# Decays of a gated delta-rule layer by a running product on VectorE, and VectorE's dependent steps in another order

## The reference

```python
q = silu(conv4(x @ Wq.T)); k, v = silu(conv4(x @ Wk.T)), silu(conv4(x @ Wv.T))   # k, v: two per token
beta = 2 * sigmoid(x @ Wb.T)
g = -exp(A_log) * softplus(x @ Wa.T + dt_bias)      # one per token and head, on the first of its two keys
q, k = l2norm(q) / sqrt(128), l2norm(k)
def step(state, inp):                                # 128 steps
    state = state * exp(g_t)
    v_new = (v_t - k_t @ state) * b_t
    state = state + outer(k_t, v_new)
    return state, q_t @ state                        # kept for the second key of a token
o = rms_norm(o) * o_norm_w * silu(x @ Wg.T)
return o.reshape(B, L, KEY_DIM) @ Wo.T
```

## Time and profile before

| | us |
|---|---|
| three runs, median | 1167.6 |
| lowest, highest | 1165.88, 1169.84 |
| profiled execution: its span | 1164.1 |

### The profile page before, as it was taken

The page is one execution under the profiler, slowest core; times in us unless marked ns, Lnnn a source line. Parts: engine busy times, 40 slices in busy tenths (PEclk is TensorE's granted clock), DMA queues, the critical chain, the costliest instruction groups (busy, mean ns, idle before and its releaser), DMA issues.

```text
span 1164.1 us, 28733 instructions
## 1 busy us (share of the span) xinstructions
PE 1114.7 (96%) x11460; PEld 768.8 (66%) x11460; DVE 821.3 (71%) x1452; ACT 703.5 (60%) x1215; POOL 501.4 (43%) x709
## 2 busy tenths in 40 slices
PE   8989799999999999999997899889999999999998
PEld 3444455555555555565554556679999899989987
DVE  5989668868868778778767665676566666565562
ACT  5767477667677676776775866645444444444443
POOL 1659475685684783883975812212000000011000
PEclk9999799999999999999999999999999999999999
DMA  4222234545545555565555642252222221111100
GB/s 124 61 54 69 69 55 78 98 98 73 117 80 75 109 82 94 103 121 123 120 84 145 190 133 75 44 175 49 52 51 52 69 52 47 47 46 48 30 20 10
DMA packets 147284, 93.74 MB, mean 81 GB/s; under 512 B 80688, under 2 KB 130736, under 8 KB 146256
## 3 DMA queue, kind: packets, MB, share of 16 engines
q1 hardware_dynamic: 146000, 91.71, 35.8%
q10 hardware_dynamic: 1152, 0.21, 0.1%
HBM read 54.77 MB, written 14.55 MB: 60 GB/s over the span
## 4 chain that ended last, share of the span: by engine, by line
PE 76%; DVE 10%; POOL 5%; ACT 4%; issue 3%; SPq 1%; DMA 1%; ACTq 0%; DVEq 0%; POOLq 0%
PE proj L535 21%; PE out L1673 5%; PE gram L550 5%; PE turned_v_chain L1673 5%; PE proj L1735 4%; PE turned_v_chain L1747 4%; DVE conv L1143 4%; PE proj L1612 4%; PE gram L1647 2%; PE turned_v_chain L541 2%; PE out L559 2%; POOL inverse L1378 2%; PE decays L566 2%; POOL rank_one L1375 2%; PE turned_v_chain L684 2%
## 5 line engine op out<-in xcount | busy, mean ns | idle before, releaser
L1143 DVE SCALAR_TENSOR_TENSOR conv<-proj,kq_weights,conv 128x504 f32<-128x504 f32 (+2 forms) x261 | 189.8, 732 | 25.8 <-ACT conv L865 19.3
L535 PE MATMUL proj<-xT,vg_weights 128*128 128x512 f32 x384 | 189.8, 618 | 4.8 <-DVE conv L1143 2.0
L1990 POOL TENSOR_TENSOR rope<-rope_part,rope_part 128x512 f32<-128x512 f32 x32 | 42.1, 1336 | 321.5 <-DVE rope_part L1921 321.5
L535 PE MATMUL proj<-xT,kq_weights 128*128 128x512 f32 x348 | 168.7, 610 | 5.4 <-DVE conv L1143 5.1
L1143 DVE SCALAR_TENSOR_TENSOR conv<-proj,vg_weights,conv 128x504 f32<-128x504 f32 (+2 forms) x192 | 140.6, 733 | 39.3 <-ACT conv L865 34.3
L1378 POOL TENSOR_TENSOR inverse<-inverse,rank_one 128x30 f32<-128x30 f32 (+14 forms) x240 | 125.5, 523 | 18.8
L1375 POOL TENSOR_TENSOR rank_one<-inverse 128x30 f32<-128x30 f32 (+14 forms) x240 | 117.2, 488 | 22.2 <-DVE inverse L1187 7.3
L535 PEld LDWEIGHTS proj<-xT,kq_weights 128*128 128x128 f32 x348 | 62.4, 190 | 80.8 <-issue 69.4
L535 PEld LDWEIGHTS proj<-xT,vg_weights 128*128 128x128 f32 x384 | 68.4, 192 | 69.2 <-issue 61.3
L550 PEld LDWEIGHTS gram<-keys_q 128*64 128x64 f32 x896 | 56.8, 136 | 42.5 <-issue 24.9
L865 ACT ACTIVATE conv<-proj,kq_weights 128x512 f32<-128x512 f32 x87 | 59.6, 685 | 41.3 <-PE proj L535 40.9
(11 more groups left out here) (263 smaller groups left out, 2471.8 us busy)
## 6 DMA issues: line engine op xcount, KB each, us to landing
kq_weights<-in_kq_w SPq DMA_DIRECT2D x32, 390.0 KB, 6.9
vg_weights<-in_vg_w SPq DMA_DIRECT2D x32, 390.0 KB, 6.2
o_scratch<-oT SPq DMA_DIRECT2D x32, 256.0 KB, 2.2
o_in<-o_scratch SPq DMA_DIRECT2D x16, 512.0 KB, 4.0
o_rs<-o_rs_quarters SPq DMA_DIRECT2D x88, 64.0 KB, 5.9
diagonal<-gram_decayed SPq DMA_DIRECT2D x128, 32.0 KB, 1.9
inverse<-inverse SPq DMA_DIRECT2D x32, 128.0 KB, 2.8
q_first<-rope SPq DMA_DIRECT2D x128, 32.0 KB, 1.9
```

Of the source, the lines that this page charges most:

```text
L535: mm = e.matmul(bank(c, u)[:], w[:, (k * 3 + c % 3) * 128:(k * 3 + c % 3 + 1) * 128], xT[g][:, k, :], start=(k == 0), stop=(k == KD - 1))
L1143: e.scalar_tensor_tensor(acc(c, u)[:, :, back:], src[:, :, 0:S - back], weights(c, u)[:, j:j + 1], acc(c, u)[:, :, back:], ALU.mult, ALU.a ...
L1990: e.tensor_tensor(turned[half][:].rearrange("p b r q -> p r b q"), parts[2 * half][:], parts[2 * half + 1][:], op).then_inc(s_turned, 1)
```

## The change

The decays are made otherwise. exp(g) of a group's tokens is made once, as rows: TensorE's `decay_rows` picks g by masks (`pick`, `since_lhs`), ScalarE's `exp_rows` takes the exponentials, SP's `store_rows` writes them to DRAM. This happens twice: for units 0 to 7 in slot 1, for all others in slot 8. For each unit SP's `load_decay` reads them back, spread over 64 partitions by each of two DMAs, and a third reads start values for the second half. VectorE's `scan_decay`, a `tensor_tensor_scan`, multiplies along the tokens: state = token_decay * state + begin. That gives EE with its zeros, so the masked copy is gone. GpSimd's `decay_low` multiplies the first half of the columns by `since`. Of the two tiles of each kind, the second stands in o_sum and o_rs while these are free, up to slot 8; from slot 8 on there is one, and its load waits for the scan before it. `decays`, `decay_steps`, `decayed_causal` and `exp_between` are gone, and with the last the two table loads in slots 2 to 7; in the loop both stay, since o_rs needs them.

```diff
@@ SP
+                def store_rows(part):
+                    e.wait_ge(s_row0, 2)
+                    e.wait_ge(s_rows, ROWS_DONE[part])
...
+                def load_decay(u):
+                    e.wait_ge(d_rows, 48 if u < H else 144)
+                    wait(e, s_scan, read_before(u))
...
                 for s in range(SLOTS):
+                    if live(ua) and s > LAG:
+                        load_decay(ua)
...
+                    if s == ROWS_SLOT:
+                        store_rows(1)
+                        load_decay(ua)
+                    if 0 < s < LAG - 2:
+                        load_decay(s + 1)
@@ TensorE, slots 1 to 8
-                    if s > 1:
-                        decays(ub)
+                    if s == ROWS_SLOT:
+                        decay_rows(1)
                     project(K0, ua)
+                    if s == 1:
+                        decay_rows(0)
                     project(K1, ua)
-                    e.wait_ge(s_conv[Q], 3 * ua)
-                    project(Q, ua)
                     e.wait_ge(s_silu[Q], ub + 1)
                     wait(e, s_gm, 4 * ub - 2)
                     gram(0, ub)
+                    e.wait_ge(s_conv[Q], 3 * ua)
+                    project(Q, ua)
@@ ScalarE, slots 1 to 8
                     tap(K1, ua)
+                    if added(K1, ua):
+                        last_tap(K1, ua)
...
+                    if s == ROWS_SLOT:
+                        e.preload_act_table_set(LN_EXP)
+                        exp_rows(1)
+                        k_norms(0)
@@ VectorE
+                def scan_decay(u):
+                    e.wait_ge(d_token[spare(u)], 48 * loads(u))
+                    wait(e, s_low, u - 1)
+                    e.tensor_tensor_scan(flat(EE[u % 2]), token_of(u)[:], begin_of(u)[:], 0.0, ALU.mult, ALU.add).then_inc(s_scan, 1)
...
+                    if full and s > LAG:
+                        conv_step(Q, ub, 1)
+                        copy_y(uc, (1,))
+                        conv_step(Q, ub, 2)
+                        copy_y(uc, (3,))
+                        conv_step(Q, ub, 3)
...
+                    if live(ua):
+                        scan_decay(ua)
@@ GpSimd
-                def decayed_causal(u):
-                def decay_steps(u):
+                def decay_low(u):
+                    e.wait_ge(s_scan, u + 1)
+                    e.wait_ge(s_rows, ROWS_DONE[0 if u < H else 1])
+                    half = EE[u % 2][:, :, 0:S // 2]
+                    some = slice(u * GB, (u + 1) * GB)
+                    e.tensor_tensor(half, half, since[:, some, None].broadcast_to([128, GB, S // 2]), ALU.mult).then_inc(s_low, 1)
+                def add_last(c, u):
+                    e.wait_ge(s_last[c], u)
+                    e.wait_ge(s_conv[c], 3 * u + 2)
+                    some = acc(c, u)[:, :, CONV - 1:]
+                    e.tensor_tensor(some, some, last[c][:, :, CONV - 1:], ALU.add).then_inc(s_conv[c], 1)
```

389 lines of the change are left out of this document (247 added, 142 removed).

## The result

The changed kernel takes 1187.1 us (median of 4 runs, 1185.2 to 1187.8), the kernel before in the same rounds 1167.6: a ratio of 1.0173, 95% interval 1.0153 to 1.0193. It is 1.7% slower, and 12 us above the upper end of my range. The profiled execution's span is 1183.1 us, 19.0 more than before.

What follows compares the result with a forecast made beforehand. TensorE was taken to be busiest in the loop, VectorE in the first slots, with V1 waiting for both. Span 1164.1 + 4.5 (start) - 6.2 (loop) = 1162.4, plus 3.5 from span to median: 1165.9 us, range 1154 to 1175.

Steps and rivals of the forecast that it cites:

- Part 5: Slots 1 to 8: VectorE 8.9 us a slot against 9.0, slot 5 starting at 66.2; 1.9 us gained by slot 9.
- Part 6: Slots 8 to 10: columns 6.2 us later, V1 of slot 10 4.5 us later net, the 1.9 us gained before included.
- Part 1: TensorE loses the decays, 1.05 us a unit; the loop won't gain 23.1 us, since V1 also waits for VectorE.
- Part 2: The new scan on VectorE: 1.10 us from start to start, with 0.6 and 2.1 as ends.
- Part 3: Normal loop slot: V1 starts 12.7 us after K1's projection instead of 13.3, a gain of 0.6 us.
- Part 4: Loop slots that turn lose 0.36 us, those that load gain 0.2; whole loop gains 6.2; SP's three loads covered.
- After slot 32: Behind the loop: nothing changes its order on the chain.
- A: Loop: copies and steps overlap on VectorE, 8.8 us more gained, 1157 us; chance 0.25.
- B: Slot 9: two scans wait for store, landing and load, each round 3 us more, 1172 us; chance 0.15.
- C: Slots 5 to 9 and loop: the scan takes longer, 1172 us at 1.5 us, 1182 at 2.1; chance 0.06.
- D: First slots: GpSimd's additions come late behind its gate series, costing 4 us, 1170 us; chance 0.12.

Runs made afterwards that it cites:

- e4: Kernel before, with the decay product of the second mask cut to one column of 512 from unit 9 on: ratio 0.9953 to the kernel before.
- e9: e7 with both copies of Y on ScalarE behind Q's tap in slots 10 to 32: 1161.0 us, ratio 0.9966 to the kernel before.
- e1: Changed kernel with the first gram round behind Q's projection on TensorE again in slots 1 to 8: ratio 1.0168 to the kernel before.
- e11: e9 with ADDED = 0, the last taps of K1 and Q in slots 1 to 4 on VectorE again: ratio 0.9986 to the kernel before.
- e2: Changed kernel with GpSimd's last six steps of the gates' series moved from slot 4 to 5, behind decay_low: ratio 1.0160 to the kernel before.
- e8: Changed kernel with ADDED = 0, the last taps of K1 and Q in slots 1 to 4 on VectorE again: ratio 1.0136 to the kernel before.
- e3: Changed kernel with the scan of slots 11 to 32 moved behind Q's last step on VectorE: ratio 1.0084 to the kernel before.
- e5: e3 with both copies of Y on ScalarE behind Q's tap in slots 10 to 32: ratio 1.0055 to the kernel before.
- e6: Changed kernel with the edits of e1, e2 and e3, the scan of slot 9 moved too: 1168.0 us, ratio 1.0012 to the kernel before.
- e7: e6 with rows made in slot 7, unit 8's scan ahead of V0's steps, the elimination's last steps later: ratio 1.0007 to the kernel before.
- e10: e9 with load_decay behind the weights of V on SP's queue in the loop: 1157.1 us, ratio 0.9932 to the kernel before.

## Why the prediction was wrong, point by point

Two steps failed. The larger one is the path of VectorE's steps through slots 1 to 9 (Parts 5 and 6): V1 of slot 10 was to be 4.5 us later and was 15.6. Counted by VectorE's first steps, the 11.1 us between are 3.7 in slots 1 to 4 (1.0 of it ahead of slot 0's tap), 3.5 in slot 5, 2.2 in slots 6 and 7, -0.6 in slot 8, 2.9 from there to the columns, and -0.7 behind them. So most of it is lost ahead of slot 8, where I had expected a gain; the stretch of slots 8 to 10, where I had placed the loss, cost 1.6 more than predicted, and that it is so little is in part luck, since the waits found there are mostly others than the one in the sum. The other step is the loop, where I put TensorE's clock and the three new loads on SP at nothing: 7.4 us. Point by point:

**Part 1, TensorE's gift isn't the gain**: right, and e4 shows its size, 5.5 us of 22.

**Part 2, the scan**: right. 1.08 us from start to start against 1.10. By the Trainium skill's half throughput ("DVE: opcode table, instruction layouts, handler registers and perf-mode slots", "Datapath and trigger behaviour") it was an estimate of 1.07; the trace agrees.

**Part 3, a normal slot**: right. From K1's projection to V1's 12.5 and 12.7 us against 12.7; the slot 20.99 instead of 21.55.

**Part 4, the slots that turn and load**: the path was right, one term was too small and two were missing. In the turning slot it is 13.9 us from K1 to V1 (14.07 predicted). In the loading slot 13.55 instead of 13.1: load and norms took 3.36, not 2.9, since the first of the norms' steps took 1.16 us instead of 0.19 (below). Without a clock fall four slots take 84.14, against 83.6. What I left out is what an idle TensorE does to its clock. I had put a wait of 1.8 us there and priced it as that wait; behind two of five such waits the clock fell, and the interval took 23.04 and 23.03 us instead of 21.41: 1.6 each. Two falls give 3.2, the loading slots 2.6 (0.53 more than predicted, five times), and the turning slots give 0.8 back (0.16 less than predicted, five times). The other 2.4 come mostly in the last cycles, where TensorE waited for DMAs (prepare_in and vg_weights, 1.8 us) that it didn't wait for before. That is the 7.4. That the cost of three more loads on SP was "covered" was the step that failed there. Its price in the changed kernel wasn't measured by itself; in the faster loop of e9, moving the loads took 2.1 us off.

**Part 5, slots 1 to 8**: wrong. Slot 5's first step came at 69.86, not 66.2. I had counted a loop of 7.7 us in which the gram round follows Q2 and GpSimd's sum, and said of slots 2 and 3 that they wait for rounds and scan, but gave this no price. What stands ahead of the round on TensorE is VectorE's reading of the unit before in the same bank, which in slot 2 needs a scan and a half product first. e1 takes the round away from there and K0's tap of slot 3 comes 3.4 us earlier. By slot 5 1.0 of it is left, 2.7 with the sums gone as well (e11, whose other edits don't bear on these slots: e9 has 56.34 there, e1 56.46), which is what these slots had lost beyond the prediction once the offset of 1.0 is taken off. Slot 5 took 15.9 us, not 12.4: I had let the wait for the diagonals go and not asked what is late next. It was GpSimd's half product, behind six steps that the sums had pushed back; e2 and e8, two different ways to clear that queue, both remove the wait and have K0's tap of slot 6 3.7 and 3.9 us earlier. Slot 6 took 10.8 instead of 8.9, with the clock low for 10.2 us from 82.4 on; in the second trace of the same kernel it was 3.4. That the clock is what slot 6 lost by is argued from these two traces; no run takes it apart.

**Part 6, slots 8 to 10**: slot 8 was right (12.3 against 12.9), and the transfers too: the start values landed 9.2 us after V0's first step, as counted. But VectorE waited for them 0.39 us, not 2.5, since K0's tap was late itself: the landing was right, and the wait was not. From V0's first step to the columns it took 18.6 us instead of 15.7. The sum had one wait of VectorE in it, of 2.5 us; there were four, for K0's tap (2.07), the start values (0.39), `decay_low` (1.04) and the gram round (1.86), 5.4 in all, and that is the 2.9. "The elimination ends at 119" was wrong as well: on GpSimd it started at 88.27 instead of 74.19, behind norms that had moved back and the half product of unit 5, and ended at 129.66. It still ended ahead of VectorE's own steps, so it wasn't what the columns waited for. From the columns to V1 it took 15.4, 16.1 were predicted.

**After slot 32**: that nothing changes there was wrong by 2.2 us. TensorE waited 3.7 us for vg_weights there, 1.7 before; in the second trace 4.8. The clock fell twice for 3.4 us between 618 and 660, before once in the same stretch of work. Why the load lands later wasn't tried.

**The rivals.** None is what happened. A (copies and steps overlap) is out by the rows above. B's chain of store, landing and load cost 0.4 us of wait. C's scan was no slower on the path. D came nearest, a late GpSimd behind its gate series, but mostly through the half product and in slot 5; the sums' own detour cost 0.9 us up to slot 5 (e8), 1.6 with the gram round moved (e11 against e9). The range was too narrow for a reason that the list shows: I took the four as cases that exclude each other, each with one loss over the same sum. The losses found lie in different slots, and they added up.

## What to carry to other kernels

Where work moves from the engine that bounds the loop to one that hands over to it, the gain is what the handover leaves; measure it by taking the work away alone. An instruction that others wait for belongs ahead of what can wait, on every in-order queue: moving the scan behind Q's steps was worth 11 us, six steps on GpSimd 3.7 at their place, three loads on SP 4. Where a new wait puts TensorE to rest, ask what its clock does behind it: at the waits of 1.4 us here it fell one time in three, for 1.6 to 1.7 us more. And losses in different places add up, so a range has to hold their sum.

## What the runs showed of the hardware

**The price of a short rest.** Five profiles (two of the changed kernel, and e1, e2, e8) each have the five waits of 1.4 us in the loop. Behind 8 of the 25 the granted clock fell for 3.4 us, which cost 1.6 to 1.7 us each. Behind e4's five waits of 1.0 us it did not fall, nor in the same slots of e3, e5, e6, e7, e9, e10 and e11, whose waits for VectorE are 0.4 us or none. The length of the rest alone doesn't decide it: of the 11 waits of 1.25 to 2.25 us for prepare_in late in the loops of e3, e5, e6, e7, e9 and e11, one was followed by a fall (e11, 2.2 us). What decides the runs don't show.

**A scan held by GpSimd, and GpSimd by a scan.** The scan reads two operands in SBUF. Of the changed kernel's 32 scans the shortest took 1.15 us and eight took 2.06 or 2.07. All eight began 0.28 or 0.29 us after GpSimd's sum of squares had started. One of them, VectorE and GpSimd:

```profile
185.87 1.27 POOL L1628 TENSOR_TENSOR o_sum<-o_sum,q_sq 128x512 f32<-128x512 f32 x1 [1.76 <-ACT o_sum L1133]
...
186.15 2.07 DVE L1236 TENSOR_TENSOR_SCAN decayed<-token_decay,begin 128x512 f32<-128x512 f32 x1
...
187.09 2.19 POOL L1635 TENSOR_TENSOR oT<-oT,o_rs 128x512 f32<-128x512 f32 x1
```

The sum takes its usual 1.27 us, the scan ends 1.08 us after it, and the next product on GpSimd, 1.27 elsewhere, takes 2.19 and ends 1.06 us after the scan: each is held until the other has ended. The Trainium skill, "SBUF — State Buffer", section "Who interferes with whom", says that a VectorE instruction with two SBUF inputs contends with a GpSimd instruction that reads SBUF, and calls the contention an exclusive lock. The trace agrees. In the slot of these rows it costs nothing: the scan ends at 188.22 and VectorE waits for Q's tap until 189.73 anyway.

The norms' first step took 0.19 us in all eight cases before and 1.15 to 1.17 in five of eight now, in the slots that load in the loop. By the line that makes it, before and then after (times in ns: shortest, median, longest), and GpSimd's and VectorE's rows at one of them:

```profile
L1174 DVE TENSOR_SCALAR n<-inverse x8: 188/188/190, 71.5 to 622.6; 128x32 f32<-128x32 f32 x8
```

```profile
L1248 DVE TENSOR_SCALAR n<-inverse x8: 179/1151/1168, 82.3 to 641.6; 128x32 f32<-128x32 f32 x8
```

```profile
231.03 1.27 POOL L1635 TENSOR_TENSOR oT<-oT,o_rs 128x512 f32<-128x512 f32 x1
231.19 1.16 DVE L1248 TENSOR_SCALAR n<-inverse 128x32 f32<-128x32 f32 x1
```

It ends as GpSimd's product does, so it is held for about 1 us, in the slot where VectorE is on the path. Before, the product of the norms two instructions behind it took 0.76 to 0.79 us in the same slots, and 0.19 now: part of this price was there already and moved.
